# Local attention: exponentials that take the maximum as bias, and projections of queries, keys and values as three float32r products of split operands

## The reference, cut to what matters

```python
h = shift_token(x)                        # x: (4, 1024, 128)
qkv = h @ wqkv                            # 128 -> 3 * 512
q, k, v = ...                             # 8 heads of 64
q = l2norm(q) * qs ; k = l2norm(k) * ksc
q, k = rotary_xpos(q, k)
# 16 windows of 64 queries, each looks at its own and the preceding window
sim = einsum('bhwid,bhwjd->bhwij', bq * 8, bk); sim = where(mask, -max, sim)
o = einsum('bhwij,bhwjd->bhwid', softmax(sim), bv)
x = x + o @ wo
...                                       # shift, layer norm, GELU-gated feed-forward
```

## Time and profile before

| | us |
|---|---|
| median of 3 runs (1561.33 to 1567.19) | 1563.13 |
| the profiled execution, its own time | 1563.58 |
| its span in the trace | 1561.7 |
| TensorE busy | 1346.8 (86%) |
| VectorE busy | 1145.6 (73%) |
| ScalarE busy | 801.7 (51%) |
| GpSimd busy | 724.0 (46%) |
| mean granted TensorE clock | 0.947 |

### The profile page before, as it was taken

The page is one execution under the profiler, slowest core; times in us unless marked ns, Lnnn a source line. Parts: engine busy times, 40 slices in busy tenths (PEclk is TensorE's granted clock), DMA queues, the critical chain, the costliest instruction groups (busy, mean ns, idle before and its releaser), DMA issues.

```text
span 1561.7 us, 39029 instructions
## 1 busy us (share of the span) xinstructions
PE 1346.8 (86%) x15968; PEld 970.4 (62%) x15968; DVE 1145.6 (73%) x2484; ACT 801.7 (51%) x1633; POOL 724.0 (46%) x562
## 2 busy tenths in 40 slices
PE   4545999988999999984999999967989999998797
PEld 3434878875777777762666666654556666665554
DVE  3776776434888888874888888864578888888565
ACT  1222223224666666653777777742457777776421
POOL 1752545541344433434666666632246666666100
PEclk7776999996999999997999999999999999999999
DMA  4000544500000000003000100011100000000011
GB/s 133 0 0 16 112 93 110 108 13 2 3 3 3 4 3 3 3 3 91 8 8 7 22 8 8 1 30 28 25 24 8 9 17 13 9 5 2 12 31 54
DMA packets 61837, 40.34 MB, mean 26 GB/s; under 512 B 41312, under 2 KB 51808, under 8 KB 61664
## 3 DMA queue, kind: packets, MB, share of 16 engines
q1 hardware_dynamic: 61664, 37.88, 10.2%
HBM read 27.12 MB, written 2.36 MB: 19 GB/s over the span
## 4 chain that ended last, share of the span: by engine, by line
PE 33%; ACT 8%; SPq 6%; DVE 4%; POOL 2%; issue 1%; DMA 1%; DVEq 0%; POOLq 0%; ACTq 0%
PE PS L1872 7%; SPq L1463 5%; PE PS L1923 5%; PE PS L1957 4%; PE PS L1914 4%; PE PS L1891 3%; PE PS L1937 2%; ACT e_oT L1787 2%; PE PS L1948 2%; ACT qk L1756 2%; ACT e_pm L1793 2%; PE PS L1907 2%; POOL rot L1537 2%; PE PS L2010 1%; PE PS L2019 1%
## 5 line engine op out<-in xcount | busy, mean ns | idle before, releaser
L1537 POOL TENSOR_TENSOR rot<-qk,sinl 128x1024 f32<-128x1024 f32 x64 | 217.6, 3401 | 139.4 <-DVE qk L1631 139.4
L1530 POOL TENSOR_TENSOR rn<-ss,neghalf 128x16 f32<-128x16 f32 x64 | 185.6, 2901 | 108.6 <-DVE ss L1624 108.6
L1756 ACT ACTIVATE qk<-PS 128x512 f32<-128x512 f32 x128 | 76.4, 597 | 135.7 <-PE PS L1872 135.7
L1102 DVE TENSOR_REDUCE d_mx<-PS 128x4 f32<-128x576 f32 x128 | 96.9, 757 | 66.3 <-PE PS L1246 63.3
L1872 PE MATMUL PS<-wqkv,hT 128*128 128x512 f32 x256 | 128.8, 626 | 10.9 <-DMA qks<-in_e_ks 5.7
L607 POOL TENSOR_TENSOR uu<-uu,cb 128x512 f32<-128x512 f32 x64 | 82.8, 1295 | 90.0 <-DVE uu L839 88.2
L1923 PE MATMUL PS<-ident,e_pm 128*128 128x128 f32 x512 | 84.5, 289 | 45.9 <-ACT e_pm L1793 44.3
L1923 PEld LDWEIGHTS PS<-ident,e_pm 128*128 128x128 f32 x512 | 55.9, 144 | 102.4 <-ACT e_pm L1793 95.7
L739 ACT ACTIVATE sg<-PS 128x512 f32<-128x512 f32 x72 | 43.0, 597 | 134.1 <-PE PS L667 133.0
L1165 ACT ACTIVATE pa<-PS 128x512 f32<-128x512 f32 x128 | 76.5, 597 | 61.8 <-PE PS L1255 61.7
L1610 DVE TENSOR_REDUCE e_mx<-PS 128x8 f32<-128x1024 f32 x64 | 78.2, 1222 | 30.7 <-PE PS L1914 30.6
(11 more groups left out here) (241 smaller groups left out, 3535.9 us busy)
## 6 DMA issues: line engine op xcount, KB each, us to landing
cb<-comb_rows SPq DMA_DIRECT2D x32, 512.0 KB, 9.1
X<-in_L_attn_x SPq DMA_DIRECT2D x4, 512.0 KB, 7.4
zs<-Z SPq DMA_DIRECT2D x64, 32.0 KB
zg<-Z SPq DMA_DIRECT2D x16, 128.0 KB
out_x<-X SPq DMA_DIRECT2D x8, 256.0 KB, 2.5
zs<-Z SPq DMA_DIRECT2D x64, 31.8 KB
zg<-Z SPq DMA_DIRECT2D x16, 127.0 KB
wqkv<-in_e_wqkv SPq DMA_DIRECT2D x2, 768.0 KB, 4.2
```

The source lines that it names most:

```text
L1102: chain(dve.tensor_reduce(mx[:, par, :, :], s, AX.X, ALU.max))
L1530: pool.tensor_tensor(rn[:, v % 2, :], ss[:, v % 2, :], c.neghalf[:, :], ALU.pow).then_inc(rn_ready.sem, 1)
L1537: pool.tensor_tensor(rot[:, :, :, :], x, bc(sinl[:, t, :, :], 2, H2), ALU.mult).then_inc(rot_ready.sem, 1)
L1756: last = act.activation(qk[:, v % 4, s, :, :].rearrange("p h e -> p (h e)"), PS[:, QBANK + s, :], ACT.Copy)
```

## The change

Three things are done in `local_transformer`.

1. The exponentials: DVE no longer subtracts the maximum. It writes the negated row maxima (`maxima`, one reduction), and ACT computes exp(score - maximum) straight from PSUM with the negated maximum as a bias for each partition. Since a bias is one number for each partition, one ACTIVATE of 512 columns becomes four of 128, for each half. ACT's order in a turn changes too: the copy of the queries, exponentials of half 0, the copy of the keys, exponentials of half 1.
2. The projections: the weights are split once for each layer into a float32r high part (ACT, `round_weights`) and the rest (DVE in layer 0, POOL in layer 1), the features into a high part (ACT, the copy that was there) and the rest (DVE, `low`). Each float32 matmul becomes three float32r ones, hi*hi, hi*lo and lo*hi, over the same 512 columns.
3. What follows from it: PE waits for `low` before it projects, and a mask and a block of zeros now lie in an older buffer (`c.hT`), to make room.

```diff
-        mask32 = ssb("e_mask32", [P, 2, KEYS2])
+        mask32 = c.hT[:, 1, 0:2 * KEYS2].rearrange("p (m k) -> p m k", k=KEYS2)
...
             def _(pool):
+                def split_weights(L, k):
+                    pool.wait_ge(whi_ready.sem, whi_ready.at(3 * L + k + 1))
+                    pool.tensor_tensor(w_lo[:, third(k)], wqkv[:, third(k)], w_hi[:, third(k)], ALU.subtract).then_inc(wlo_ready.sem, 1)
...
                         if L + 1 < DEPTH and g < 3:
                             tables(L + 1, g)
+                            split_weights(L + 1, g)
                         if g + 2 < G:
                             rstd(L, g + 2)
...
             def _(dve):
-                def shift(L, v):
+                def low(L, v):
+                    dve.wait_ge(eh_ready.sem, eh_ready.at(n(L, v)))
+                    dve.tensor_tensor(h_lo[:, v % 4, :], PS[:, QBANK, 0:P], h_hi[:, v % 4, :], ALU.subtract).then_inc(el_ready.sem, 1)
+
+                def maxima(L, v):
                     dve.wait_ge(s_ready.sem, s_ready.at(n(L, v)))
+                    if n(L, v) > 2:
+                        dve.wait_ge(p_exp.sem, p_exp.at(2 * (n(L, v) - 2)))
                     s = PS[:, SBANK:SBANK + 2, :].rearrange("p r (j k) -> p r j k", k=2 * W2)
-                    steps(dve.tensor_reduce(mx[:, :, :], s, AX.X, ALU.max))
-                    for h in range(2):
-                        if n(L, v) > 2:
-                            dve.wait_ge(pT_psum.sem, pT_psum.at(2 * (n(L, v) - 2) - 1 + h))
-                        dve.tensor_tensor(pm[:, v % 2, h, :, :, :], s[:, :, 2 * h:2 * h + 2, :],
-                                          bc(mx[:, :, 2 * h:2 * h + 2], 3, 2 * W2), ALU.subtract).then_inc(p_shifted.sem, 1)
+                    dve.tensor_reduce(mx[:, v % 2, :, :], s, AX.X, ALU.max, negate=True).then_inc(max_ready.sem, 1)
...
                 def attend(L, u):
+                    if has(u + 4) and (u >= 0 or L == 0):
+                        low(L, u + 4)
                     if has(u):
-                        shift(L, u)
+                        maxima(L, u)
...
                 dve.wait_ge(qkv_loaded.sem, qkv_loaded.at(16 * 3))
+                for k in range(3):
+                    dve.wait_ge(whi_ready.sem, whi_ready.at(k + 1))
+                    dve.tensor_tensor(w_lo[:, third(k)], wqkv[:, third(k)], w_hi[:, third(k)], ALU.subtract).then_inc(wlo_ready.sem, 1)
                 dve.wait_ge(consts.sem, 48)
...
                     for g in range(G):
+                        if L + 1 < DEPTH and lead(g) is not None:
+                            low(L + 1, lead(g) + 4)
                         gated(L, g, 0)
...
             def _(act):
+                def round_weights(L, k):
+                    if k == 0:
+                        act.wait_ge(qkv_loaded.sem, qkv_loaded.at(16 * 3 * (L + 1)))
+                        if L:
+                            act.wait_ge(ev_psum.sem, ev_psum.at(nunits * L))
+                    act.activation(w_hi[:, third(k)], wqkv[:, third(k)], ACT.Copy).then_inc(whi_ready.sem, 1)
...
                 def exponent(L, v, h):
-                    act.wait_ge(p_shifted.sem, p_shifted.at(2 * n(L, v) - 1 + h))
-                    p = pm[:, v % 2, h, :, :, :].rearrange("p r j k -> p (r j k)")
-                    act.activation(p, p, ACT.Exp).then_inc(p_exp.sem, 1)
+                    if h == 0:
+                        act.wait_ge(max_ready.sem, max_ready.at(n(L, v)))
+                    if n(L, v) > 2:
+                        act.wait_ge(pT_psum.sem, pT_psum.at(2 * (n(L, v) - 2) - 1 + h))
+                    for r in range(2):
+                        for j in range(2):
+                            at = 2 * h + j
+                            last = act.activation(pm[:, v % 2, h, r, j, :], PS[:, SBANK + r, at * KEYS2:(at + 1) * KEYS2], ACT.Exp,
+                                                  bias=mx[:, v % 2, r, at:at + 1])
+                    last.then_inc(p_exp.sem, 1)
...
                     if has(u + 4):
                         if u >= 0 or L == 0:
                             features(L, u + 4)
-                        take_features(L, u + 4)
+                        take_features(L, u + 4, 0)
                     if has(u):
                         exponent(L, u, 0)
+                    if has(u + 4):
+                        take_features(L, u + 4, 1)
+                    if has(u):
                         exponent(L, u, 1)
                         take_p(L, u, 0)
...
                         gelu(L, g, 2)
+                        if L + 1 < DEPTH and g < 3:
+                            round_weights(L + 1, g)
...
             def _(pe):
+                def project(to, v, k):
+                    pe.matmul(to, h_hi[:, v % 4, :], w_hi[:, third(k)], start=True, stop=False)
+                    pe.matmul(to, h_hi[:, v % 4, :], w_lo[:, third(k)], start=False, stop=False)
+                    return pe.matmul(to, h_lo[:, v % 4, :], w_hi[:, third(k)], start=False, stop=True)
+
                 def project_qk(L, v):
-                    pe.wait_ge(eh_ready.sem, eh_ready.at(n(L, v)))
-                    if v == 0:
-                        pe.wait_ge(qkv_loaded.sem, qkv_loaded.at(16 * 3 * (L + 1)))
+                    pe.wait_ge(el_ready.sem, el_ready.at(n(L, v)))
                     for s in range(2):
-                        pe.matmul(PS[:, QBANK + s, :], h_of(v), wqkv[:, s * INNER:(s + 1) * INNER],
-                                  start=True, stop=True).then_inc(eqkv_ready.sem, 1)
+                        if v == 0:
+                            pe.wait_ge(wlo_ready.sem, wlo_ready.at(3 * L + s + 1))
+                        project(PS[:, QBANK + s, :], v, s).then_inc(eqkv_ready.sem, 1)
```

More of the change, by code:

```diff
@@ L1367, in local_transformer @@
         sinl = ssb("sinl", [P, TB, 2, DH2])
-        mask32 = ssb("e_mask32", [P, 2, KEYS2])
+        mask32 = c.hT[:, 1, 0:2 * KEYS2].rearrange("p (m k) -> p m k", k=KEYS2)
         mask = ssb("e_mask", [P, 2, KEYS2], BF16)
-        zero = ssb("zero", [P, B, half])
+        zero = c.hT[:, 0, 0:B * half].rearrange("p (b d) -> p b d", d=half)
         zs = ssb("zs", [P, B, D])
@@ L1433, in lead, with third @@
             return g - 7 if 3 <= g <= 6 else None
-        def h_of(v):
-            return c.hT[:, v % 2, P * (v // 2 % 2):P * (v // 2 % 2 + 1)]
+        def third(k):
+            return slice(k * INNER, (k + 1) * INNER)
         with nc.Block() as block:
@@ L1750, in features, with take_features @@
                     act.wait_ge(zsT_psum.sem, zsT_psum.at(n(L, v)))
-                    act.activation(h_of(v), PS[:, QBANK, 0:P], ACT.Copy).then_inc(eh_ready.sem, 1)
-                def take_features(L, v):
-                    for s in range(2):
-                        act.wait_ge(eqkv_ready.sem, eqkv_ready.at(2 * n(L, v) - 1 + s))
-                        last = act.activation(qk[:, v % 4, s, :, :].rearrange("p h e -> p (h e)"), PS[:, QBANK + s, :], ACT.Copy)
-                    last.then_inc(qk_taken.sem, 1)
+                    act.activation(h_hi[:, v % 4, :], PS[:, QBANK, 0:P], ACT.Copy).then_inc(eh_ready.sem, 1)
+                def round_weights(L, k):
[4 more added lines that the diff above has]
+                    act.activation(w_hi[:, third(k)], wqkv[:, third(k)], ACT.Copy).then_inc(whi_ready.sem, 1)
+                def take_features(L, v, s):
+                    act.wait_ge(eqkv_ready.sem, eqkv_ready.at(2 * n(L, v) - 1 + s))
+                    act.activation(qk[:, v % 4, s, :, :].rearrange("p h e -> p (h e)"), PS[:, QBANK + s, :],
+                                   ACT.Copy).then_inc(qk_taken.sem, 1)
                 def squares(L, v):
-                    act.wait_ge(qk_taken.sem, qk_taken.at(n(L, v)))
+                    act.wait_ge(qk_taken.sem, qk_taken.at(2 * n(L, v)))
                     if n(L, v) > 1:
@@ L1834, in gelu @@
                        .then_inc(gelu_ready.sem, 1)
+                for k in range(3):
+                    round_weights(0, k)
                 for L in range(DEPTH):
@@ L1881, in project_v @@
                         pe.wait_ge(resid.sem, resid.at(nunits * L))
-                    pe.matmul(PS[:, VBANK, :], h_of(v), wqkv[:, 2 * INNER:3 * INNER],
-                              start=True, stop=True).then_inc(ev_psum.sem, 1)
+                    if v == 0:
+                        pe.wait_ge(wlo_ready.sem, wlo_ready.at(3 * L + 3))
+                    project(PS[:, VBANK, :], v, 2).then_inc(ev_psum.sem, 1)
                 def turn_qk(L, v):
```

19 lines of the change are left out of this document (11 added, 8 removed).

## The result

The changed kernel takes 1573.58 us (median of 5 runs, 1572.11 to 1578.23) against 1562.95 us of the kernel before (5 runs beside it, 1560.78 to 1567.19). The ratio is 1.0070, 95% interval 1.0047 to 1.0093: slower by 0.5 to 0.9%. The profiled execution took 1572.67 us. The forecast was 1573 us.

A forecast was written before the change was run, and what follows sets the result against it. The prediction took the path through PE's projection and the ACT queue behind it as the bound, with POOL's 9.18 us loop as floor. Profiled 1563.6 + 3.7 for turns + 5.8 for the start = 1573.1 us, range 1558 to 1590.

The forecast's parts named there:

- the likeliest case: In the last stage, an exponential piece takes between 0.24 and 0.28 us, giving 1564 to 1582 us; chance 0.62.
- ACT's queue sets the turn: In the last stage's loop, copies and eight pieces on ACT delay the second `turn_p`, making a turn 9.93 us.
- The term of the turn: Last stage's loop: second `turn_p` at T+4.70 instead of T+4.63, +0.07 us a turn, 53 turns, 3.7 us.
- with 0.06 for the semaphore: Handover from ACT's `take_p` to PE's second `turn_p`: 0.06 us, from T+4.64 to T+4.70.
- The piece: One 128-column exponential with bias on ACT: lasts 0.37 us, takes 0.26 of the queue, bounds 0.17 and 0.37.
- the 0.11 of the long GELU: Overlap in ACT's queue, from a GELU with bias lasting 0.69 us with its successor starting 0.58 later.
- The rival that rested on it: Exponential pieces on ACT overlap less: 1590 us at 0.30 a piece, 1620 at 0.37; chance 0.15.
- `low` costs nothing in a turn: DVE's `low` before PE's projection: done at 809.57, 0.31 us to spare, no cost while DVE is free.
- The start: Front of layer 0: `low` behind the tables and PE's low clock delay it by 5.8 us, between 5.1 and 6.4.
- some tenths: Front of layer 0: `low(1)` ahead of the first sum of squares and `low(2)` ahead of the first `norm` add this.
- only the first six products run at half speed: Front of layer 0: six projection products at PE's low clock take about 2.6 us.
- The rest, at nothing: Layer 1's split and front, layers' last tiles and a late `low` once: these cancel within about 1 us.

The follow-up runs named there:

- e1: The changed kernel with the float32 projections of before, keeping the new exponentials and ACT's new order: 1574.58 us, ratio 1.0063 to the kernel before.
- e5: The changed kernel with the bias left out of its exponentials, the four pieces of a half kept: 1537.7 us (one run).
- e6: The changed kernel with one maximum for all eight heads of a query, so one exponential instruction a half: 1530.6 us, ratio 0.9785 to the kernel before.
- e2: The changed kernel with only its projections: subtraction on DVE, one exponential a half, ACT's old order: 1561.3 us, ratio 0.9976 to the kernel before.
- the second pair: Later traces of the kernel before and the changed kernel, both unchanged: 1565.64 and 1576.24 us (one run each).
- e8: The changed kernel with unread transposes in PE's first four waits of layer 0 (24, then ten each): 1572.56 us, ratio 1.0044 to the kernel before.
- e11: The changed kernel run once more, unchanged, for a second trace: 1576.24 us (one run).

## Why the prediction was right, point by point

**The whole.** 1573 was forecast, 1573.58 measured, and the likeliest case is the one that happened. But that the sum is right to a microsecond is luck, because errors cancel: in the first trace the turns cost 4.6 us more than forecast and the front 2.8 more, and some 7 us came back that I had at nothing.

**ACT's queue sets the turn: shown.** e1 has the exponentials alone, e5 and e6 take the price away and the turn falls at once to the next bound. The offsets in the timeline, with T = 799.05: pieces of half 0 at T+1.49 (predicted 1.47), keys' copy T+2.49 (2.51), half 1 T+2.97 (3.00), `take_p` T+3.97 (4.04). It lasts 0.67 rather than 0.60, so it ends at T+4.64, exactly as forecast.

**The term of the turn was mis-sized: 0.07 to 0.085 was 0.156.** The step that failed is one number, "with 0.06 for the semaphore". The second `turn_p` starts 0.15 us behind `take_p`'s end (803.69 to 803.84), of which the chain counts 0.14 as issue. The 0.06 is what stands between the exponentials and the first `turn_p` (801.68 to 801.74). The earlier trace rows has the distance for the very pair of instructions: `take_p` ends at 804.50 and `turn_p` starts at 804.65. Other transposes stood ahead of it on PE there, so that row proves nothing, but it was nearer than the one that I took. 0.09 x 53 = 4.8 us. Why one handover takes 0.06 and the other 0.15 isn't settled.

**The piece: 0.26 forecast, 0.25 measured**, 0.16 without the bias. The overlap in a queue is not the 0.11 of the long GELU but 0.396 - 0.25 = 0.15; the piece itself is longer than I had (0.396 against 0.37), and the two errors cancel. ScalarE: Activation LUTs of the Trainium skill, section What ACT_TABLE_LOAD costs, gives as an estimate 0.39 for the instruction, where the row has 0.396, and 0.29 in a queue, where the trace has 0.25. The page's duration holds and its overlap of 93 ns is too small for these pieces. The rival that rested on it did not happen.

**`low` costs nothing in a turn: right.** DVE is free at that point, as forecast (idle for 0.58 us ahead of it), and 0.35 us of cover are left where I had 0.31. e2 shows what it hangs on: with the subtractions still on DVE the low part is the last link to the projection.

**The start was mis-sized: 5.8 was 8.6 at the third mask (7.1 in the second pair as it stands, 8.6 there too from the cast of the mask on).** The first part held: the first sum of squares moved by 5.2. The failed step is "some tenths" for `low(1)` and `low(2)`, and with it the assumption that only the first six products run at half speed. In the first trace those of the first four tiles do (0.43 against 0.23 each, nine a tile), and `low(2)` passes the delay on to the norm: POOL's root was done at 731.43, and the norm started at 733.73, 2.3 us later. e8 prices the clock at 3.1 us of the third mask's delay. TensorE: Matmul & The Clock Gate of the Trainium skill, section What's actually happening, says that the throttled state is the default and that activity lifts it; the windows of before, after and e8 (0.83, 0.50 and 0.92 in the first) agree.

**"The rest, at nothing" was too high by about 2 us, and more in the first trace.** In one of the last tiles of a layer, the third from the end, DVE was the one behind. Before, scores that ended at 1025.96 met their maximum only at 1027.15; after, the maximum starts 0.07 after the scores' end (1038.39):

```profile
1024.86 1.10 PE L1914 MATMUL PS<-e_kT,e_qT 64*64 64x128 f32 x32
1027.15 1.19 DVE L1610 TENSOR_REDUCE e_mx<-PS 128x8 f32<-128x1024 f32 x1
```

```profile
1037.29 1.10 PE L1955 MATMUL PS<-e_kT,e_qT 64*64 64x128 f32 x32
1038.46 1.22 DVE L1624 TENSOR_REDUCE e_mx<-PS 128x8 f32<-128x1024 f32 x1
```

I had compared only the exponentials there and left DVE's queue out. From this tile's mask to the next it is 11.89 us before and 10.35 after (10.61 in the second trace). In the next tile DVE is no earlier after the change: the maximum starts 0.91 us after the scores' end, before 0.62. That tile is 1.0 us shorter in the first trace all the same (10.09 against 11.14), with a granted clock of 1.00 against 0.85, and not shorter in the second (11.14 at 0.85). So the first trace's further give-back there goes with PE's clock and not with the change; what came back between the layers is scatter by e11.

**What stays open.** Why the two handovers from ACT to PE differ; and why the 3 us won in e8's front come out in its total as 1 us of the median, with an interval that does not settle it. Of the front, the share of the order on DVE (up to 5.5 us) wasn't tried with the clock held up. The keys' copy between the two halves wasn't tried at another place in ACT's order, so its part in the turn is argued from the offsets alone.

## What to carry to other kernels

An operation that is folded into another as its bias is free only where the folded instruction isn't cut up for it. Here one maximum a head made eight instructions of two, the bias cost 0.09 us in each, and one maximum for a whole row gave 2% where the change as made lost 0.7%. (It needs heads whose scores are of like size: a head far below the row's maximum loses its exponentials to underflow.) Before making matrix work cheaper, ask which queue ends the turn and what the new operands need at the start: the products won 0.23 us a turn alone and 0.15 beside the pieces, and gave 7 to 8 us back in a front where PE waited and its clock stayed down. When carrying a handover time into a sum, take it from the same pair of instructions.

## What the runs showed of the hardware that was not expected

- A bias costs its 0.09 us in ScalarE's queue too: pieces of 128 columns with a bias last 0.396 us and follow each other every 0.25; without a bias 0.319 and 0.16. It is the distance that counts, not the duration shown: `take_p` (512 columns) behind the pieces shows 0.67 us where it showed 0.60 before, but its successor starts 0.48 us later (803.02, 803.50), as behind a copy of 0.60.
- Filling PE's waits with 54 transposes moved the granted clock of the front's two windows from 0.50 and 0.50 (0.50 and 0.73 in a second trace) to 0.92 and 0.91, and the first mask came 3.0 us earlier than in the trace of the kernel without them that began its front at the same time, the third mask 3.1. Filling only the first wait (24 transposes) gave 0.81 and then 0.53 in the two windows.
- The same program had 0.50 or 0.73 in the front's second window in two executions. A DMA that landed 1.3 us earlier in one of them moved its whole front by as much (third mask at +60.90 and not +62.19).
